# Cross-attention scores of a decoder layer: three passes of split operands or two, with heads interleaved in a 32-row tile

## The reference, cut to what matters

```python
x = x + self_attention(layernorm(x))
h = layernorm(x)
q = (h @ Wq).reshape(B, S, H, D).transpose(0, 2, 1, 3)
k, v = split(ctx @ Wkv)                      # 375 context tokens
scores = einsum('bhsd,bhkd->bhsk', q, k) + rel_bias[buckets]
x = x + merge(softmax(scores) @ v) @ Wo
x = x + experts(layernorm(x))                # top 2 of 8
```

## Time and profile before

| what | value |
|---|---|
| median of 3 runs | 1312.01 us (1311.14 to 1312.11) |
| the profiled execution, its own time | 1313.93 us |
| its span, first to last instruction | 1312.3 us |
| mean granted TensorE clock | 0.971 |
| busy: PE, PEld, DVE, ACT, POOL | 1230.8, 1092.4, 872.0, 728.3, 856.2 us |
| cross scores (L613) | from 46.4 to 884.3 us, 1536 matmuls |

### The profile page before, as it was taken

One profiled execution on the slowest core, in us unless ns is written; L12 is line 12 of the kernel. 1 busy time (PEld: TensorE's weight loads), 2 busy tenths in 40 slices (PEclk: granted clock), 3 DMA queues, 4 the chain that ended last, 5 costly groups with the idle time before them and its releaser, 6 DMA issues. The chain is left out here.

```text
span 1312.3 us, 40150 instructions
## 1 busy us (share of the span) xinstructions
PE 1230.8 (94%) x13828; PEld 1092.4 (83%) x13829; DVE 872.0 (66%) x3949; ACT 728.3 (55%) x1828; POOL 856.2 (65%) x1597
## 2 busy tenths in 40 slices
PE   6999999999999999999999999993599999999993
PEld 4788888888888888888888888872499999999992
DVE  3567788877888788778878788876244444444441
ACT  2456666666666666666666666661344444444440
POOL 4677887878788787877778787765244444444431
PEclk8899999999999999999999999996699999999997
DMA  9600111101110111101101111001585222222224
GB/s 163 132 21 21 35 38 37 28 28 38 44 28 28 35 33 42 28 28 39 43 28 28 32 31 40 13 23 46 175 208 122 49 48 48 48 48 48 49 38 128
DMA packets 44276, 70.15 MB, mean 53 GB/s; under 512 B 6928, under 2 KB 30992, under 8 KB 44048
## 3 DMA queue, kind: packets, MB, share of 16 engines
q1 hardware_dynamic: 27936, 42.60, 12.2%
q0 software_dynamic: 15744, 25.31, 10.1%
q10 hardware_dynamic: 432, 0.10, 0.0%
HBM read 46.90 MB, written 24.75 MB: 55 GB/s over the span
## 5 line engine op out<-in xcount | busy, mean ns | idle before, releaser
L481 POOL TENSOR_SCALAR arena<-arena,mC 112x375 f32<-112x375 f32 x512 | 299.2, 596 | 116.1 <-DVE mC L889 115.8
L889 DVE CUSTOM_DVE_ANT_0 arena<-bank_S,arena 112x375 f32<-112x375 f32 x512 | 265.0, 543 | 90.8 <-PE bank_S L613 64.0
L1131 POOL DMA_INDIRECT acc<-y,xb x64 | 119.3, 1865 | 206.9 <-DVE y L1275 170.2
L487 POOL TENSOR_SCALAR arena<-arena,mF 112x112 f32<-112x112 f32 x512 | 176.8, 362 | 23.3 <-DVE mF L877 21.5
L771 ACT ACTIVATE pTC<-bank_Q 126x336 f32<-126x336 f32 x286 | 128.5, 449 | 48.8 <-PE bank_Q L623 47.6
L735 ACT ACTIVATE arena<-bank_B 128x224 f32<-128x224 f32 (+5 forms) x229 | 87.3, 381 | 110.4 <-PE bank_B L542 36.7
L1262 DVE SCALAR_TENSOR_TENSOR hT<-bankU,gub,gate 128x128 f32<-128x128 f32 x256 | 72.2, 345 | 107.8 <-PE bankU L1171 93.7
L735 ACT ACTIVATE arena<-bank_A 128x224 f32<-128x224 f32 (+3 forms) x219 | 82.1, 375 | 96.8 <-PE bank_A L636 29.6
L623 PE MATMUL bank_Q<-ident,arena 112*126 112x112 f32 x858 | 130.9, 261 | 0.5 <-ACT pTC L771 0.5
L1171 PE MATMUL bankG<-xbT,gwb 128*128 128x128 f32 x1024 | 126.6, 277 | 1.0 <-ACT gwb L1218 1.0
L1212 ACT ACTIVATE xbT<-bankX 128x256 f32<-128x256 f32 x64 | 24.5, 383 | 181.2 <-PE bankX L1159 181.2
(11 more groups left out here) (207 smaller groups left out, 2930.5 us busy)
## 6 DMA issues: line engine op xcount, KB each, us to landing
arena<-in_l_ctxT SPq DMA_DIRECT2D x32, 378.0 KB, 3.6
xb<-xs POOLq DMA_DIRECT2D x64, 129.0 KB, 3.5
arena<-in_L_ffn_gate_w SPq DMA_DIRECT2D x8, 512.0 KB
arena<-in_L_ffn_up_w SPq DMA_DIRECT2D x8, 512.0 KB
arena<-in_L_ffn_down_w SPq DMA_DIRECT2D x8, 512.0 KB
arena<-in_x SPq DMA_DIRECT2D x32, 112.0 KB, 2.2
acc<-arena SPq DMA_DIRECT2D x32, 112.0 KB, 1.9
out<-acc SPq DMA_DIRECT2D x4, 896.0 KB, 9.2
```

The source lines that it names most:

```text
L481: pool.tensor_scalar(z[n % NZ][:, 0:T], z[n % NZ][:, 0:T], -1.0, mC[:, n:n + 1], ALU.mult, ALU.add).then_inc(s_u, 1)
L487: m = pool.tensor_scalar(sF[r][:, j, :], sF[r][:, j, :], -1.0, mF[:, r, j:j + 1], ALU.mult, ALU.add)
L889: dve.tensor_tensor_reduce(out=z[n % NZ][:, 0:T], in0=bank[f"S{r}"][0:S, 0:T], in1=nbias[:, n, :], scale=1.0, scalar=3.0e38, op0=ALU.add, ...
L1131: pool.indirect_dma_start(out=acc[:, :], out_offset=bass.IndirectOffsetOnAxis(ap=xb[x][:, D + 1:D + 2].bitcast(I32), axis=0), in_=y2[x % 2 ...
```

## The change

The heads of a pair are no longer stacked as 16 + 16 rows of a tile but interleaved, the first head on even partitions and the second on odd ones (through the host's permutation of the weights' columns and the half mask). For each head there is then a tile of its own, 32 rows full: on its own parity the queries (or keys) that the projection left there, on the other parity a copy moved over by one partition. For the keys, one parity holds the high part and the other the low part; for the queries both parities hold the same part. One matmul over 32 rows gives query part x (key high + key low), and two passes, query high and query low, give the whole sum. The fourth product, low x low, which was left out before, is now in it.

The moved copies are made by transfers, issued on SP as two new steps: `kx` (2 transfers a batch, 64 partitions x 2 runs x 1504 B each) once `k0` and `k1` are drained, and `qx` (2 transfers, 64 partitions x 4 runs x 448 B each) once `q2` is drained. `cross_scores` waits for both. ScalarE writes each high part of the keys twice. The low keys go into one new buffer, `k2_low`, that isn't doubled; its writer waits for the transfer of the batch before. The order of all steps is a new one.

```diff
-    half_mask[np.arange(P), np.arange(P) // DH % 2] = -1.0
+    half_mask[np.arange(P), np.arange(P) % 2] = -1.0
 PERIOD = """
-rs1@3 sT0@3 e15@-1 t15 u14@-1 pv2@1 u12@-1 q2l@1 t14 t12 ln1@4 e13@-1 x3@-2 k1c@1 u13@-1 st@-2 t13 rcB@-2 t2@1
-t1@1 t3@1 e3 oc3@-1 xn@3 km@2 u1 u3 t0@1 x3Tc@-2 u2 Lc@2 rs3@-2 e2 pfD@-2 onc@1 pv1@1 e1 t4@1 e0 S0@2 cl@2
-k0c@1 t6@1 e7 t5@1 nrm@2 oncc@-1 e6 t7@1 k1l@2 pf@-1 u0 oc0 u6 u4 u7 u5 sc@-3 e4 p14@1 re@-2 xn2@1 u8 v0@2 e9
-e10 x2Tc@1 Lx@5 sT1@3 p12@1 e8 S1@2 pvS@3 u9 xTc@3 u10 u11 e5 v@4 rs2@1 p15@1 q2m@1 p13@1 qkc@3 e11 ot@3 t11@1
-t10@1 k1@3 sE2@2 nrmc p3@2 t8@1 pv3@1 t9@1 v1c@1 S2@2 k0l@2 sE3@2 x1@2 x3T p2@2 su3@2 ln2@2 oc2 on@3 sm3@3
-p1@2 otc@1 lg@-1 sE0@2 su2@2 p0@2 oc1 sm2@3 k0@3 x2 sm1@3 sm0@3 wo@3 p7@2 p6@2 su0@2 u15 ln3 onC@1 S4@4 pv0@2
-rcA@-1 e14 v0c@1 sE1@2 rt p4@2 woc@1 p9@2 p10@2 ch@2 x2T@3 xT@5 p8@2 p5@2 e12 oTc@2 q2@3 S3@2 qk@5 p11@2 sT2@4
-v1@3 vc@3 sT3@4 su1@2
+t10 Lc@1 rs3@-1 kx ln1@4 u14 u15 u13 woc@-2 t11 p6@-1 lg@-2 t9 e13 q2l@1 k1c@2 x2@-1 ln3@-1 e12 t14 t13 S3@-1
+t12 t15 u2@1 u0@1 rcA@-2 v0 t0@1 su3@3 e3@1 t2@1 nrm@2 xn2@2 t3@1 qkc@4 p8@-1 sE3@3 oc3 sE2@3 e0@1 x3Tc@-1
+x2Tc@2 t1@1 cl@2 u12 e7@1 sm3@3 u3@1 sm2@3 p11@-1 pv0@-1 pvS@1 sm0@3 S0 p10@-1 p9@-1 ot@1 v@2 su2@3 rs2@2 e4@1
+u7@1 sm1@3 v1c@2 u6@1 oncc e1@1 p14@-1 sE1@3 re@-1 pv1@-1 S4@2 u1@1 on@1 x1@2 p15@-1 xT@3 ln2@2 t7@1 p2 pv2@-1
+q2m@2 e5@1 wo@1 k0@1 k0l@2 t6@1 u4@1 t5@1 t4@1 sE0@3 e6@1 k1l@2 v0c@2 pfD@-2 su1@3 S1 su0@3 p13@-1 k1@1 p12@-1
+p3 qk@3 t8@1 ch@3 pf@-3 sT3@2 e8@1 oc0@1 rcB@-2 u5@1 qx sT2@2 e11@1 u8@1 sc@-2 oTc@3 pv3@-1 e10@1 S2 Lx@5 e9@1
+x3 p0 vc@4 km@4 e14@1 x3T@-2 p7 rs1@5 x2T@1 p4 u11@1 oc1@1 xn@5 otc@-1 onc@3 v1@1 p1 e15@1 onC@-1 sT1@2 rt@-2
+xTc@5 q2@1 u10@1 oc2@1 p5 st@-2 e2@2 sT0@2 u9@1 nrmc k0c@3
 """
-            q2 = [[s1(f"q2_{part}{i}", [P, DC, 2, S], F32R) for part in ("high", "low")] for i in range(2)]
-            k2 = [[s1(f"k2_{part}{i}", [P, DC, T + 1], F32R) for part in ("high", "low")] for i in range(2)]
+            q2 = [s1(f"q2_{i}", [P, 2, DC, 2, S], F32R) for i in range(2)]
+            k2 = [s1(f"k2_{i}", [P, DC, 2, T + 1], F32R) for i in range(2)]
+            k2_low = s1("k2_low", [P, DC, T + 1], F32R)
+                        elif step == "kx":
+                            drained_wait(sp, "k0", b)
+                            drained_wait(sp, "k1", b)
+                            for p in range(2):
+                                sp.dma_start(k2[b % 2][1 - p:P:2, :, p, :].bitcast(F32),
+                                             k2_low[p:P:2, :, :].bitcast(F32)).then_inc(s_kx[b % 2], 16)
+                        elif step == "qx":
+                            drained_wait(sp, "q2", b)
+                            for p in range(2):
+                                sp.dma_start(q2[b % 2][1 - p:P:2, :, :, p, :].bitcast(F32),
+                                             q2[b % 2][p:P:2, :, :, p, :].bitcast(F32)).then_inc(s_qx[b % 2], 16)
                     def cross_scores(g, b, F_):
-                        if g == 0:
-                            drained_wait(pe, "q2", b)
-                        drained_wait(pe, f"k{g // 2}", b)
-                        c, k = g // 2, g % 2
-                        for u, w in PASSES:
+                        need(pe, s_qx[b % 2], 32 * (b // 2 + 1))
+                        need(pe, s_kx[b % 2], 32 * (b // 2 + 1))
+                        c, p = g // 2, g % 2
+                        for u in range(2):
                             for r in range(HG):
-                                m = pe.matmul(bank[f"S{r}"][0:S, 0:T + 1], q2[b % 2][u][32 * r:32 * r + 32, c, k, :],
-                                              k2[b % 2][w][32 * r:32 * r + 32, c, :],
-                                              start=(u, w) == PASSES[0], stop=(u, w) == PASSES[-1])
+                                m = pe.matmul(bank[f"S{r}"][0:S, 0:T + 1], q2[b % 2][32 * r:32 * r + 32, u, c, p, :],
+                                              k2[b % 2][32 * r:32 * r + 32, c, p, :], start=u == 0, stop=u == 1)
                     def halves(b):
-                            m = act.activation(q2[b % 2][0][:, :, p, :], v3(B_, DC, S), ACT.Copy, scale=hmask[:, p:p + 1])
+                            m = act.activation(q2[b % 2][:, 0, :, p, :], v3(B_, DC, S), ACT.Copy, scale=-1.0)
                     def keys_high(o, b):
-                        act.activation(k2[b % 2][0][:, o, :], B_[:, 0:T + 1], ACT.Copy).then_inc(s_kh, 1)
+                        for p in range(2):
+                            m = act.activation(k2[b % 2][:, o, p, :], B_[:, 0:T + 1], ACT.Copy)
+                        m.then_inc(s_kh, 1)
                         elif step == "q2l":
-                                m = dve.scalar_tensor_tensor(q2[b % 2][1][:, :, p, :], v3(bank[place["q2", b][0]], DC, S), hmask[:, p:p + 1],
-                                                             q2[b % 2][0][:, :, p, :].bitcast(F32), ALU.mult, ALU.subtract)
+                                m = dve.scalar_tensor_tensor(q2[b % 2][:, 1, :, p, :], v3(bank[place["q2", b][0]], DC, S), -1.0,
+                                                             q2[b % 2][:, 0, :, p, :].bitcast(F32), ALU.mult, ALU.subtract)
                         elif step in ("k0l", "k1l"):
-                            dve.tensor_tensor(k2[b % 2][1][:, o, :], bank[place[f"k{o}", b][0]][:, 0:T + 1],
-                                              k2[b % 2][0][:, o, :].bitcast(F32), ALU.subtract).then_inc(drain_sem(f"k{o}", b), 1)
+                            if b:
+                                need(dve, s_kx[(b - 1) % 2], 32 * ((b - 1) // 2 + 1))
+                            dve.tensor_tensor(k2_low[:, o, :], bank[place[f"k{o}", b][0]][:, 0:T + 1],
+                                              k2[b % 2][:, o, 0, :].bitcast(F32), ALU.subtract).then_inc(drain_sem(f"k{o}", b), 1)
-    c, r, p, d = np.meshgrid(np.arange(2), np.arange(HG), np.arange(2), np.arange(DH), indexing="ij")
+    c, r, d, p = np.meshgrid(np.arange(2), np.arange(HG), np.arange(DH), np.arange(2), indexing="ij")
```

More of the change, by code:

```diff
@@ L326, in decoder_layer @@
             s_kh = sem("cross_keys_high_ready")
+            s_kx = [sem("cross_keys_paired0"), sem("cross_keys_paired1")]
+            s_qx = [sem("cross_queries_paired0"), sem("cross_queries_paired1")]
             NLATE = 8
@@ L749, in halves @@
                         B_ = filled_wait(act, "q2", b)
-                        if b == 0:
-                            act.wait_ge(s_mask, 32)
-                        elif b >= 2:
+                        if b >= 2:
                             filled_wait(act, "S3", b - 2)
                         for p in range(2):
-                            m = act.activation(q2[b % 2][0][:, :, p, :], v3(B_, DC, S), ACT.Copy, scale=hmask[:, p:p + 1])
+                            m = act.activation(q2[b % 2][:, 0, :, p, :], v3(B_, DC, S), ACT.Copy, scale=-1.0)
                         m.then_inc(s_qh, 1)
```

## The result

| | before | after |
|---|---|---|
| median | 1311.7 us (4 runs) | 1301.56 us (1300.18 to 1303.01, 4 runs) |
| ratio | | 0.9923, 95% interval 0.9906 to 0.994 |
| profiled execution, its own time | 1313.93 | 1300.18 |
| its span | 1312.3 | 1298.4 |

The kernel is faster, by 10 us where 26 were forecast. Two later jobs gave the same kernel ratios of 0.99 and 0.9909 (e5, e11), so 10 to 13 us. The 3.8 us between it and the 10.1 of the medians come from which executions were profiled.

What follows compares the result with a forecast made beforehand. TensorE's own work in its written order was taken to set the pace, 26.93 us a batch. -22 - 8 + 3 = -27 from the profiled 1313.9 gave 1287, stated as a median of 1286; forecast 1279 to 1292, range 1279 to 1308.

Steps and rivals of the forecast that it cites:

- the ends: Before the first and after the last scores: work moved ahead and one exposed query transfer (3.6) cost +3 us.
- the new order in the loop: TensorE's steps with other neighbours: 0.27 us less a batch, -8 us over roughly 30 periods, bounds 0 and -12.
- The removed pass: Four score steps a batch, each without a middle pass of 0.17 us: 0.69 a batch, -22 us over 32 batches.
- the named wait: Self values behind S1 wait for VectorE's router ranks: 0.54 us instead of 0.27, gone in the new order.
- the short form: Period of a batch in the new order: 26.94 less 0.69 (passes) less 0.27 (wait) gives 25.98 us.
- the prediction's allowance of 0.1: In the summed TensorE sequence: 0.1 us more where a step of another tile shape follows.
- The queries' transfer: Query pair ahead of S0: lands in 3.6 us, in time by 0.6; price 0, ends 0 and 1.7 a batch.
- the lower bound of 2.8: Landing time of the query pair priced by bytes, 2.8 us; by packets it was 4.5 or 5.9.
- (a): Rival: query transfers take 4.5 to 5 us, S0 waits 0.3 to 0.8 each batch; 1295 to 1310 us; chance 0.2.
- (c): Rival: short runs make the query pair land after 5.9 us, S0 late by 1.7; slower, 1338 us; chance 0.08.
- ScalarE's second key copies: Two more copies a batch, 0.48 us each, ScalarE 17.6 to 18.6 of 26; price 0 while in time for banks.

Runs made afterwards that it cites:

- e5: The changed kernel run again unedited, in the second job; 1300.72 us, ratio 0.99 to the kernel before.
- e11: The changed kernel run again unedited, in the third job; 1301.52 us, ratio 0.9909 to the kernel before.
- e8: The changed kernel with the low queries' pass issued twice, so three passes again; 1323.14 us, 22.4 above the changed kernel in the same job.
- e6: The kernel before with the new order alone, three passes, no kx or qx; 1317.16 us, ratio 1.0029 to the kernel before.
- e7: The changed kernel with the old order, kx and qx put in behind Lx; 1330.19 us, ratio 1.0125 to the kernel before.
- e12: e9 with rcB moved to directly ahead of pfD in VectorE's order; 1294.62 us, ratio 0.9865 to the kernel before.
- e10: The changed kernel with input 3 and context 1 loaded before the bias, expert 0's package after input 6; 1297.18 us, ratio 0.9875 to the kernel before.
- e9: e10 with the four transfers of batch 0 issued from ScalarE's DMA queue instead of SP's; 1294.36 us, ratio 0.9854 to the kernel before.

## Why the prediction was wrong

By its own steps, in spans. Two terms failed: the ends (+3 for what measured +10.8), and the size of the new order in the loop (-8 for about -3).

- **The removed pass, -22: right.** 0.17 per step by the earlier trace rows, 0.53 long steps after, and e8 gives 22.4 us for putting one back. The rule on the drain (the Trainium skill, "TensorEngine Tiling (Array Packing)", Key Properties) was of use there: the skill says that a change of the tiling mode drains TensorE. The trace agrees: 0.53 is left of 0.70 without the middle pass, so the two ends cost what they did.
- **The new order of TensorE, -8: the named wait was right, the rest of the term wrong.** The wait of the self values is gone. But the period is 26.13 and not 25.98, and e6 shows the order worth 0.12 a batch with three passes, not 0.27. The step that failed is the short form, 26.94 - 0.69 - 0.27, which puts all other changes of neighbours at nothing. Step against step over one period of either timeline (from 422.09 and from 416.62), the score steps fell from 3.09 to 2.13, which is the passes and the wait; everything else rose from 23.84 to 24.00. The keys took 0.19 more: in the new order S1 follows k0, which takes 1.31 (423.72 to 425.03) where the keys took 1.12 each in front of untiled steps. The sixteen transposes of heads took 0.35 more and those of the self scores 0.09; the projections gave back 0.26, `qk` and `pf` 0.09 each. A sum over like pairs has to match what follows as well as the step, and the prediction's allowance of 0.1 for it was half of what k0 needed. Over 26 full periods 0.15 is 3.8 us; the first and last ones gained less than a full period's worth, 1.5 in all.
- **The queries' transfer, 0: right in the loop of the profiled execution.** The pair was in 2.7 after its first issue, at the lower bound of 2.8, and no score step of the loop waited for it. Two transfers of 112 KB in 448 B runs landed as fast as the input load of 112 KB in 1 KB rows (2.1 and 2.2), so the prices of (a) and (c) don't hold as a rule. The rule on short runs (the Trainium skill, "DMA: Bandwidth & Descriptors", Specifications), by which the engines read, modify and write below 512 B, cost nothing here that the trace could show. But a pair now and then takes 4.0 to 5.0 (three times in e7 and in e12, twice in e8), and the cover is 4.6; in e12 that made S0 late three times. The prediction took one time for the pair and had no spread in it.
- **ScalarE's second key copies, 0: right in this order.** In e7 the bank of the keys drains late and costs 0.38 us a batch, where the order leaves no room. The cover to be named was the distance from k0 and k1 to the next fill of their bank.
- **Ends, +3: wrong, and the larger miss.** The exposed first transfer was given its landing time in the quiet loop, 3.6; it took 7.4. The start has another state: 2.6 MB of bias keep the DMA engines busy until 45.4, then the expert's package until about 52, and every later issue stands behind them. The prediction read the earlier trace rows as a mean over the span and didn't open the first 50 us. There it would have found the second thing that it put at nothing: VectorE's `ln1` of batch 3 waits for input 3 until 46.8, and in the new order the low query copies stand behind it. That alone puts S0 at 50.6 (4.2 us, e6, of which about 0.8 is the self values at the granted clock of 0.50), and the transfer at 55 to 56 (5 us more). Together 8.9. The edits of the start gave back 6.1 to 6.7 of S0's delay (e10, e9). Behind the loop 1.9 were lost. No step of the prediction looked at `rcB`, which stands 0.9 us in the way; the distance from `pf` to the experts is longer by 1.4, and e12 gets all of that back. From the last scores to `pf` 0.3 were gained, and inside the experts 0.9 more were lost, about what executions of one kernel differ by there (after, e5 and e11: 0.8).

The misses add up: 5.9 at the start, 5.3 between, 1.9 behind, 13.1 of the 27. The time fell into the range because rival (a) had stretched it, which is no credit to the range: the loss of (a)'s size came from places that no rival named.

## What to carry to other kernels

A change to a software-pipelined loop has three prices: the period, the way to the first period, and the way out; the last two are read in their own stretches, at the load that the queues have there, and each step of the new order that stands ahead of the first critical one is looked up with its own data's landing. What a shorter step frees is only worth what the tightest wait behind it lets through: two passes with their transfers were worth 16 us in one order (e6 to e5) and cost 17 in another (before to e7). And a transfer's cover is held against its slowest landings, not its median.

## What the runs showed that was not expected

- ScalarE's copy of 128 x 224 took 0.444 us with a scale from a column and 0.356 with a constant; VectorE's counterpart fell from 0.446 to 0.382. That is 0.3 us a batch on the way to the transfer.
- SP itself stood still while issuing: 6.15 us for one load of 128 KB at 32.32 and 5.93 for the next input, against 0.33 in the loop.
- The same query transfer, in the quiet loop, landed 2.1 after its issue nearly always and 3.4 to 4.4 now and then (three batches each of e7 and e12, two of e8). The cause isn't known. One such wait of 1.4 us in e7 was followed by 5 us at a granted clock of 0.66.
- ScalarE started one and the same copy either 0.04 or about 0.8 us after its data, by job and not by kernel. An order with 0.4 us of margin behind such a copy pays 0.46 each time.
